# A graph network on one core: TensorE's pieces in another order, with the ring of banks, the evictions and the last pairs reordered to match

## What is computed

```python
# layer 0
h = relu(layernorm(x))
x = x + (adj @ (h @ W0) + b0)
# layer 1, 8 heads of 256 features
h = relu(layernorm(x))                                # "feats"
p = (h @ fc_w + fc_b).reshape(..., 8, 256)            # per head
logits = (p @ q_w + q_b) + (p @ k_w + k_b).T          # a column plus a row
masked = leaky_relu(logits + (1 - adj) * -1e9, 0.01)
out = softmax(masked) @ p                             # 128 x 128 times 128 x 256, each head
x = x + sigmoid(concat(out) @ fp_w + fp_b + h)
```

## Time and profile before

| | before |
|---|---|
| time, median of 3 runs | 1424.37 us (1424.36 to 1426.49) |
| time of the profiled execution | 1423.27 us |
| its span, first to last instruction | 1421.5 us |
| granted TensorE clock, mean share of full speed | 0.998 |
| PE busy | 1400.3 us, 99% |
| DVE busy | 1262.0 us, 89% |
| ACT busy | 1111.6 us, 78% |
| POOL busy | 1105.7 us, 78% |

### The profile page before, as it was taken

The page is one execution under the profiler, slowest core; times in us unless marked ns, Lnnn a source line. Parts: engine busy times, 40 slices in busy tenths (PEclk is TensorE's granted clock), DMA queues, the critical chain, the costliest instruction groups (busy, mean ns, idle before and its releaser), DMA issues.

```text
span 1421.5 us, 32663 instructions
## 1 busy us (share of the span) xinstructions
PE 1400.3 (99%) x9624; PEld 1289.0 (91%) x9624; DVE 1262.0 (89%) x4536; ACT 1111.6 (78%) x3428; POOL 1105.7 (78%) x1291
## 2 busy tenths in 40 slices
PE   8989999999999999999999999999999999999997
PEld 7889999999999999999999999999999999999976
DVE  7988989989989989998999999999999999899875
ACT  4868787787788787787887877887887887877764
POOL 4778778778878778778778778788788788788754
PEclk9999999999999999999999999999999999999999
DMA  6213223223133133133133133232232232232111
GB/s 224 106 61 106 72 85 104 65 90 104 57 98 104 52 103 104 52 104 103 53 104 95 61 104 88 67 104 82 73 104 77 78 104 74 82 104 72 48 49 49
DMA packets 43245, 123.13 MB, mean 87 GB/s; under 512 B 5968, under 2 KB 9680, under 8 KB 43216
## 3 DMA queue, kind: packets, MB, share of 16 engines
q1 hardware_dynamic: 42928, 122.77, 27.6%
q10 hardware_dynamic: 288, 0.01, 0.0%
HBM read 105.46 MB, written 17.30 MB: 86 GB/s over the span
## 4 chain that ended last, share of the span: by engine, by line
PE 92%; DVE 3%; DMA 1%; issue 1%; ACT 1%; POOL 1%; SPq 0%; POOLq 0%; DVEq 0%; ACTq 0%
PE gbank L404 45%; PE ybank L404 24%; PE bank L404 10%; PE tbank L521 7%; PE bank L449 4%; PE bank L479 2%; DVE att L881 1%; DMA late<-fc_wT_dram 1%; PE gbank L424 1%; PE bank L457 1%; DVE att L888 0%; DVE g_lo L864 0%; ACT att L1300 0%; DVE pT_lo L871 0%; POOL att L1624 0%
## 5 line engine op out<-in xcount | busy, mean ns | idle before, releaser
L1300 ACT ACTIVATE att<-att 128x128 f32<-128x128 f32 x1024 | 397.8, 392 | 48.4 <-DVE att L888 48.3
L1617 POOL TENSOR_TENSOR att<-late,t_pos 128x512 f32<-128x512 f32 x256 | 331.4, 1296 | 131.6 <-PE tbank L521 127.7
L404 PE MATMUL gbank<-m_hi,hT_lo 128*128 128x512 f32 (+1 forms) x1024 | 404.9, 395 | 0.4 <-DVE g_lo L864 0.4
L404 PE MATMUL gbank<-m_hi,hT_hi 128*128 128x512 f32 (+1 forms) x1024 | 373.4, 365 | 0.0
L404 PE MATMUL gbank<-m_lo,hT_hi 128*128 128x512 f32 (+1 forms) x1024 | 372.4, 364 | 0.0
L1624 POOL TENSOR_TENSOR att<-att,rinv 128x512 f32<-128x512 f32 x256 | 295.2, 1153 | 94.4 <-DVE rinv L893 94.3
L864 DVE TENSOR_TENSOR g_lo<-gbank,g_hi 128x512 fp32r<-128x512 f32 x448 | 302.2, 677 | 51.1 <-ACT g_hi L1293 46.5
L881 DVE TENSOR_SCALAR_CACHE_REDUCE att<-att,kq_sb 128x128 f32<-128x128 f32 x1024 | 291.1, 338 | 33.4 <-POOL att L1617 33.4
L1293 ACT ACTIVATE g_hi<-gbank 128x512 fp32r<-128x512 f32 x448 | 259.7, 594 | 50.2 <-PE gbank L404 50.2
L1307 ACT ACTIVATE pT_hi<-tbank 128x512 fp32r<-128x512 f32 x256 | 152.9, 597 | 142.2 <-PE tbank L521 139.1
L404 PE MATMUL ybank<-g_hi,pT_lo 128*128 128x256 f32 x889 | 249.7, 281 | 3.1 <-DVE g_lo L864 2.4
(11 more groups left out here) (123 smaller groups left out, 2860.5 us busy)
## 6 DMA issues: line engine op xcount, KB each, us to landing
late<-key_rows SPq DMA_DIRECT2D x128, 512.0 KB, 6.1
g_in<-graph_dram SPq DMA_DIRECT2D x64, 512.0 KB, 3.4
out_dram<-ends SPq DMA_DIRECT2D x63, 256.0 KB, 4.5
att<-fc_wT_dram SPq DMA_DIRECT2D x4, 256.0 KB, 5.8
late<-fp_w_dram SPq DMA_DIRECT2D x4, 256.0 KB, 5.5
ends<-fp_w_dram SPq DMA_DIRECT2D x2, 512.0 KB, 7.7
late<-fc_wT_dram SPq DMA_DIRECT2D x2, 512.0 KB, 9.4
key_rows<-rows SPq DMA_DIRECT2D x64, 8.0 KB, 1.4
```

The lines of the kernel that those rows point to most:

```text
L404: mm = pe.matmul(out_ap, w, m, start=first and n == 0, stop=last and n == len(terms) - 1)
L1300: e = act.activation(a[:, s], a[:, s], ACT.Exp, scale=-1.0, bias=a[:, CH + h:CH + h + 1], accum_out=esum[j][c][:, h:h + 1])
L1617: gp.tensor_tensor(a, keys[q][:, j, c * HC:(c + 1) * HC, :], t_pos[q][:, j, :].unsqueeze(1).broadcast_to([P, HC, P]), ALU.add)\
```

## The change

No instruction is added or removed. On TensorE:

- In each step `project(i, q, A0)` goes ahead of `attend(i-1, 1, 0)`; the two attended sums of graph 1 follow each other, and `turn_keys(i+1)` comes behind both.
- B1 changes places with SIXTH and B2: the order was SIXTH, B2, `transform`, B1 and is B1, SIXTH, `transform`, B2. So SIXTH stands between a piece of 512 columns and `transform`.
- `RING` follows: B1, SIXTH and B2 move to other banks.
- In `finish` the pieces of pairs 61 to 63 are put in another order.

On DVE `key_rows_out(i+1)` moves behind `add_feats(i-1)`, and the evictions and the softmax of the last pairs are reordered. ACT evicts B1 ahead of SIXTH, and its last pairs are reordered. The diff, cut to its core:

```diff
-RING = ((B0, -1), (A1, 0), (A2, 0), (THERE, 1), (A0, 0), (SIXTH, 0), (B2, 0), (B1, 0))
+RING = ((B0, -1), (A1, 0), (A2, 0), (THERE, 1), (A0, 0), (B1, 0), (SIXTH, 0), (B2, 0))
...
@@ TensorE, step
                 last_head(i + 1, (q + 1) % U, 1)
+                project(i, q, A0)
                 attend(i - 1, (q + 2) % U, 1, 0)
+                attend(i - 1, (q + 2) % U, 1, 1)
                 turn_keys(i + 1, (q + 1) % U)
-                project(i, q, A0)
-                attend(i - 1, (q + 2) % U, 1, 1)
                 transpose_p(i, 0, 0)
+                project(i, q, B1)
                 sixth_heads(i, q)
-                project(i, q, B2)
                 transform(i + 2, (q + 2) % U)
                 transpose_p(i, 0, 1)
-                project(i, q, B1)
+                project(i, q, B2)
                 attend(i, q, 0, 0)
@@ TensorE, finish (pair 61 with 62 and 63 ahead)
                 last_head(62, 2, 1)
+                project(61, 1, A0)
                 attend(60, 0, 1, 0)
                 transpose_p(61, 0, 0)
                 attend(60, 0, 1, 1)
-                project(61, 1, A0)
                 turn_keys(62, 2)
+                project(61, 1, B1)
                 transform(63, 0)
                 sixth_heads(61, 1)
+                transpose_p(61, 0, 1)
                 project(61, 1, B2)
-                transpose_p(61, 0, 1)
-                project(61, 1, B1)
                 attend(61, 1, 0, 0)
...
                 project(62, 2, A1)
-                attend(61, 1, 1, 0)
                 transpose_p(61, 1, 1)
+                project(62, 2, A2)
                 h_ready(63)
                 last_head(63, 0, 0)
-                project(62, 2, A2)
+                last_head(63, 0, 1)
+                project(62, 2, A0)
+                attend(61, 1, 1, 0)
                 attend(61, 1, 1, 1)
-                last_head(63, 0, 1)
+                turn_keys(63, 0)
                 transpose_p(62, 0, 0)
-                turn_keys(63, 0)
-                project(62, 2, A0)
+                project(62, 2, B1)
                 sixth_heads(62, 2)
+                transpose_p(62, 0, 1)
                 project(62, 2, B2)
-                project(62, 2, B1)
-                transpose_p(62, 0, 1)
                 project(62, 2, B0)
                 attend(62, 2, 0, 0)
                 transpose_p(62, 1, 0)
                 attend(62, 2, 0, 1)
                 project(63, 0, A1)
+                transpose_p(62, 1, 1)
                 project(63, 0, A2)
-                transpose_p(62, 1, 1)
...
@@ DVE, step
                 g_low(i, A1)
-                key_rows_out(i + 1)
                 mask_min(i, q, 1, 0)
                 inverse(i, 0, 1)
                 g_low(i, A2)
                 ah_rest(i + 2, (q + 2) % U)
                 add_feats(i - 1, (q + 2) % U)
+                key_rows_out(i + 1)
...
@@ ACT, step
+                g_high(i, B1)
                 g_high(i, SIXTH)
-                g_high(i, B1)
...
@@ ACT, finish
                 exp(61, 0, 1)
+                last_high(62, 2, 1)
                 pT_high(61, 0, 0)
+                g_high(61, A0)
                 exp(61, 1, 0)
-                last_high(62, 2, 1)
-                g_high(61, A0)
```

More of the change, by code:

```diff
@@ L579, in begin @@
                 turn_keys(1, 1)
+                project(0, 0, B1)
                 sixth_heads(0, 0)
-                project(0, 0, B2)
                 aggregate(3, 0)
@@ L584, in begin @@
                 output_bias()
-                project(0, 0, B1)
+                project(0, 0, B2)
                 project(0, 0, B0)
@@ L603, in begin @@
                 turn_keys(2, 2)
+                project(1, 1, B1)
+                transpose_p(1, 0, 1)
                 sixth_heads(1, 1)
-                transpose_p(1, 0, 1)
                 project(1, 1, B2)
-                project(1, 1, B1)
                 attend(1, 1, 0, 0)
@@ L623, in begin @@
                 turn_keys(3, 0)
-                sixth_heads(2, 2)
+                project(2, 2, B1)
                 transpose_p(2, 0, 0)
                 transform(4, 1)
+                sixth_heads(2, 2)
                 project(2, 2, B2)
-                project(2, 2, B1)
                 transpose_p(2, 0, 1)
@@ L645, in begin @@
                 transpose_p(3, 0, 0)
+                project(3, 0, B1)
+                aggregate(5, 2)
                 sixth_heads(3, 0)
-                aggregate(5, 2)
                 project(3, 0, B2)
-                project(3, 0, B1)
                 transpose_p(3, 0, 1)
@@ L733, in finish @@
                 attend(62, 2, 1, 1)
+                project(63, 0, B1)
                 sixth_heads(63, 0)
+                transpose_p(63, 0, 1)
                 project(63, 0, B2)
-                transpose_p(63, 0, 1)
-                project(63, 0, B1)
                 attend(63, 0, 0, 0)
@@ L1165, in finish @@
                 inverse(61, 0, 1)
+                add_feats(60, 0)
                 key_rows_out(62)
-                add_feats(60, 0)
                 pT_low(61, 0, 0)
@@ L1190, in finish @@
                 pT_low(61, 1, 1)
+                leaky(62, 0, 1)
+                inverse(62, 0, 0)
                 keys_queries(63, 0, 0)
                 last_low(63, 0, 0)
-                leaky(62, 0, 1)
-                inverse(62, 0, 0)
+                keys_queries(63, 0, 1)
                 g_low(62, A1)
+                g_low(62, A2)
                 mask_min(62, 2, 1, 1)
                 add_feats(61, 1)
+                key_rows_out(63)
+                last_low(63, 0, 1)
                 leaky(62, 1, 0)
-                g_low(62, A2)
-                keys_queries(63, 0, 1)
-                last_low(63, 0, 1)
                 g_low(62, A0)
-                key_rows_out(63)
                 leaky(62, 1, 1)
@@ L1504, in finish @@
                 pT_high(61, 1, 1)
+                g_high(62, A2)
                 last_high(63, 0, 0)
+                last_high(63, 0, 1)
                 exp(62, 0, 1)
-                g_high(62, A2)
-                last_high(63, 0, 1)
                 pT_high(62, 0, 0)
```

## The result

The changed kernel takes 1434.43 us (median of five executions, 1430.67 to 1436.59) against 1424.73 us before (five executions beside it): a ratio of 1.0062, 95% interval 1.0044 to 1.0080, so 9.7 us slower where 2.7 us less was forecast. The profiled execution of after is the longest of its five (1436.59 us), so its trace shows 13.3 us more of span than before. The five differ with their mean clock: spans of 1428.9 and 1430.0 us at 0.997, 1434.4 at 0.993.

What follows compares the result with a forecast made beforehand. PE was taken to bound the kernel, busy 200.00 of 200 us in the middle, so only the ends could gain: -1.5 (last keys) - 1.4 (clock) + 0.2 (given back) = -2.7 us from the median, 1421.7 us; range 1418.2 to 1424.6.

Steps and rivals of the forecast that it cites:

- `begin`, taken as 0: In `begin`, B1, SIXTH and B2 change places; evictions have time to spare and PE's long waits stay: 0 us.
- Steady state, PE's work, taken as 0: In the 57 steps, the mix of 1.37 and 1.42 us groups stays as it is: 0 us.
- The rival that the short groups go: In the steps, no 256-column group is short: +1.9 us, so 1423.5 us; chance 0.22.
- The bounds: PE's work in the steps: none short, 1.9 us more; two more short in every step, 5.7 us less.
- Steady state, waits, 0: In the steps, B1, SIXTH and the keys' copy, at most 3.0 us late, cause no PE wait: 0 us.
- The 1.4 us of room: In the steps, worst case: `normalise(i-1, 1, 1)` ends at 615.6 and PE takes that attention at about 617.
- `attend(61, 0, 1)` 2.1 us late: At pair 61 in the end, SIXTH ends 2.2 us later, so this attend moves from 1366.17 to 1368.25.
- Last keys copied 1.5 us sooner: In the end, the last pair's keys are copied at 1380.2 instead of 1381.71: gain 1.5 us.
- The clock holds at the end: Behind the last keys, full clock saves 1.25 us of `attend(62, 0, 1)` and 0.17 of A1, together 1.4 us.
- The argument from 2.03 us without harm: PE idled 2.03 us at 84.15 with the clock at 1.00, so 2.5 us with four transposes should hold it.
- The rival on the slower side: Keys miss `mask_keys` in every step, `normalise(i-1, 1, 1)` is late: 0.1 us a step, 5.7 us, 1427.4 us; chance 0.08.

Runs made afterwards that it cites:

- e1: Changed kernel with ScalarE's and VectorE's evictions in `begin` put in TensorE's new order (B1, SIXTH, B2): 1432.51 us, ratio 1.0048.
- e12: Kernel before the change with only `sixth_heads(2, 2)` moved ahead of `turn_keys(3)` in `begin`: 1416.43 us, ratio 0.9985.
- e17: Changed kernel with one swap in the step, `transpose_p(i, 0, 0)` ahead of `turn_keys`, so B1 stands right behind `turn_keys`: 1426.11 us, ratio 1.0011.
- e5: e1 plus, on GpSimd behind the loop, `normalise(58, 1, 0)` ahead of the two `mask_keys` of pair 59: 1430.54 us, ratio 1.0046.
- e2: Changed kernel with TensorE's old order in `begin` (SIXTH, B2, B1) on the new ring of banks: 1434.14 us, ratio 1.0066.
- e7: e6 plus, on VectorE in `finish`, `g_low(61, SIXTH)` ahead of `pT_low(61, 0, 1)`: 1422.94 us, ratio 0.9997.
- e6: e5 plus, on TensorE in `finish`, `transform(63)` ahead of `project(61, B1)`: 1423.98 us, ratio 1.0001.
- e10: e7 plus `project(2, B1)` ahead of `turn_keys(3)` in `begin` and, on GpSimd, `normalise(58, 1, 1)` ahead of `inputs(61)`: 1419.61 us, ratio 1.0007.
- e11: Changed kernel with only `transform(63)` ahead of `project(61, B1)` in `finish`: 1429.21 us, ratio 1.0077.
- e18: e16 plus, on TensorE in `begin`, `project(3, A0)` ahead of `last_head(4)`: 1411.70 us, ratio 0.9903.
- e16: e10 plus one swap in the step, `transpose_p(i, 0, 0)` ahead of `turn_keys`: 1413.94 us, ratio 0.9922.
- e4: Changed kernel with the whole of `finish` as before on TensorE, VectorE and ScalarE, on the new ring: 1432.79 us, ratio 1.0056.

## Why the prediction was wrong, step by step

In short: four places were priced at nothing or too low, `begin`, the pace of the steps, the order of GpSimd behind the loop and the new stall at pair 61, and the gain that was forecast for the last keys did not come.

- **`begin`, taken as 0: wrong, the largest miss in the profiled execution.** The step said that the evictions "have time to spare there". TensorE's order was changed and ScalarE's list was not, so ACT waited 1.39 us at the head of its queue for a piece that now comes later, with an `exp` behind it (e1). It cost 3.2 us of waiting, and 4.0 of clock in that execution; the clock's part was less in the other traces with this `begin`.
- **Steady state, PE's work, taken as 0: wrong by 1.5 us.** The rival that the short groups go is what happened, and its price of +1.9 was near. The bounds were laid around the mix of one execution, though: beside executions of before like those around e12 the same loss is about 7 us. The reason given, that the pace hangs on what stands before a group, was right: with B1 right behind `turn_keys` (e17) the changed kernel wins some 7 us.
- **Steady state, waits, 0: right in the loop** (PE busy for 200.00 of 200) **and wrong behind it.** The 1.4 us of room (1.2 by the rows, which move the copy by 3.2 us and not 3.0) was worked out for GpSimd's order in the loop; `finish` has another, and PE waited 1.49 us once (e5).
- **`attend(61, 0, 1)` 2.1 us late: undersized.** From `last_head(62)` it came at 22.3 us instead of 17.6, 4.7 late. `g_low(A1)` came 0.6 us earlier, as said. The rest is two things that were left out: a wait of 2.05 us is itself an occasion for the clock to fall (1.6 us until SIXTH, by e2, where it held), and the `leaky` of pair 62, pushed onto `mask_keys`, took 1.70 us instead of 0.70 (start, us, line):

```profile
1379.27 1.70 DVE L888 SCALAR_TENSOR_TENSOR att<-att 128x516 f32<-128x516 f32 x1
```

- **Last keys copied 1.5 us sooner: wrong.** The copy starts 35.5 us behind `last_head(62)` instead of 32.8. The order could do it: in e7 it is 28.5.
- **The clock holds at the end: right in the profiled execution** (`attend(62, 0, 1)` took 1.60 us at full clock), **and by luck:** of the 14 traces with this order of the end it held in 9 and fell beside this `attend` in 5 (e5, e6, e10, e11, e18). Two falls ahead of it cost more than this one saved. The argument from 2.03 us without harm was an argument from one draw. The Trainium skill ("TensorE: Matmul & The Clock Gate", "What's actually happening") says that the gate's windows do not start with the kernel; that the same 2.05 us went both ways agrees with it.
- **The rival on the slower side** (keys missing `mask_keys` in each step) did not come; the loss came from places priced at nothing.

## What to carry to other kernels

When one engine's order changes, change the lists of the engines that consume its results in the same places, in the written-out head and tail as in the loop, and move with it what waits for it (the copy behind `turn_keys`: 42 us if not). A blocked instruction of your own making is to be filled with the next ready work, for each wait of about 2 us on TensorE is also a draw on its clock. Where TensorE is the bound and has no wait, read its pace from several executions, group by group: neighbours that cost no gap can still be worth 0.13 us a step.

## What was not expected of the hardware

- **Two paces of TensorE at one clock.** 12 matmuls of 256 columns took 1.37 or 1.42 us with the granted clock at 1.00 throughout: in a short group each started 113 or 114 ns after the one before it, in a long one 117 to 119. Moving `turn_keys` (16 rows) from ahead of `transpose_p` to right ahead of a 512 column piece brought the shorter pace for the groups behind that piece (e16, e17).
- **VectorE against GpSimd.** `leaky` (one tensor in SBUF read twice) takes 0.69 us, and 1.70 to 1.78 when GpSimd had begun `mask_keys` or `inputs` 0.07 to 0.53 us ahead of it (two in 3.45 us after the change, 1.30 with e1). Not every overlap costs that much: beside the GpSimd work of the loop it takes 0.7 to 0.9. The Trainium skill ("SBUF — State Buffer", "SBUF: two separate sides") has it that a VectorE operation with two SBUF inputs and a GpSimd operation that reads SBUF lock one pair of ports against each other; these rows agree with it.
- **The clock is a draw, not a threshold.** In the traces it fell beside the 2.04 us before `turn_keys(3)` in 3 of 13, beside the 2.05 before `project(61, B1)` in 4 of 6, and beside the 2.08 to 2.10 before `attend(61, 0, 1)` in 6 of 6; at the 3.53 us before `last_head(3)` it fell after the change and held in e4. A fall at the start of a group stretched it from 1.65 us to as much as 2.9.
